# Turns, logits and turned gates of two expert mixtures as 64x64 products, and their second biases inside the chunk sums

## The chip, the cores and the metric

The kernel runs on one core of one Trainium2 chip. The metric is the device time of one launch in microseconds (us), given as the median of several runs. Engines: PE is TensorE, DVE is VectorE, ACT is ScalarE, POOL is GpSimd, SP is SyncE, which issues most of the DMAs.

## What is computed

Two layers on 8 sequences of 1056 tokens (1024 image tokens and 32 text tokens) of width 64: a token embedding, an attention, a first mixture of experts, a recurrent memory ("recall") in place of an attention, and a second mixture of experts. The change is in the mixtures. Layer normalisation of the input precedes each, and the result is added to the input:

```python
gate_scores = jnp.einsum('bsd,ed->bse', x, Wg) + bg
topk_scores, topk_idx = jax.lax.top_k(gate_scores, K)          # K = 2
topk_probs = jax.nn.softmax(topk_scores, axis=-1)
combine = jnp.sum(topk_probs[..., None] * jax.nn.one_hot(topk_idx, E, dtype=x.dtype), axis=-2)
for e in range(E):
    h = jax.nn.relu(jnp.einsum('bsd,hd->bsh', x, W1[e]) + b1[e])
    y = jnp.einsum('bsh,dh->bsd', h, W2[e]) + b2[e]
    out = out + combine[..., e:e + 1] * y
```

The first mixture has E = 16 experts with 128 hidden values, the second E = 8 with 256; the first has the same form, with a normalisation behind it. The last input column is replaced by ones inside the kernel, so that the gate's bias and b1 are the last row of the folded weights. b2 is weighted by the gates, as y is.

## The kernel before

`all_stages` runs the stages in order. `moe_phase` builds a mixture; its names begin with d_ in the first and n_ in the second. Each mixture treats its 8 sequences ("batches") one after another, and each batch in three chunks of 352 tokens (CH). For a chunk the kernel goes through pairs of experts; a pair sits on the two halves of 64 partitions. A unit is one pair, chunk and hidden half of 128: DVE scales the turned tokens by the gates (`scale`, line 1617, into xg), PE makes the hidden values in p_z (`first`, line 1375: four 64x64 products with 352 columns), ACT applies the relu (`relu`, line 1474), PE adds the output into p_y over the eight units of a chunk (`second`, line 1389: again four 64x64 products). A group is two units: `first(i)`, then `second(i - 1)`. A batch has 24 units, 12 groups, and a mixture 96 groups. z(i) below is the first product of group i's `first`. All of it is f32. Behind the last unit of a chunk ACT copies half of p_y into yT (`copy_sum`, line 1481) and DVE adds the other half (`add_half`, line 1602); the next chunk's `second` waits for that.

Between the groups stand the "misc" steps, which share the banks p_g and p_l. Their order is written out by hand: FIRST_GROUP, TURNS, LOGITS, RANK, CHOOSE, KEEP, BIAS_GROUP and OUT_GROUP give the group of each step, `misc_use` numbers them, and a step waits on misc_free until the one before it has been read out, and signals misc_full. On PE a step comes before `first` of its group. For batch b + 1, while batch b is computed, and counted by groups within a batch:
- groups 8, 9, 10: `turn` (line 1334) turns the normalised tokens, which ACT has copied twice side by side (`double`, line 1446), by one 128x128 transpose for each of the nine tiles of 128 tokens, four, four and one of them; ACT copies them into xd (`untangle`, line 1454).
- group 11: `logits` (line 1343), nine products of 64x128 with E columns; DVE ranks in group 0 (`rank`, lines 1539 to 1548), chooses in groups 1 and 2 (`choose`, lines 1554 to 1572).
- group 3: `turn_gates` (lines 1349, 1350), two transposes; ACT keeps the turned gates in cT and cT_text (`keep_gates`), SP writes them to DRAM and reads them back spread over partitions (`spread_out`, `spread_in`, line 1268).
- groups 4 and 5: `turn_out` (line 1364) turns yT of the batch before, five and four transposes; DVE adds the two halves of each to the rows (`add_out`, line 1591).
- group 6: `weigh_biases` (lines 1355, 1356), the turned gates times a block matrix of b2, 512 columns on the whole array and one small product for the text rows; DVE adds that to the rows (`add_biases`, lines 1578, 1579).
DVE also measures and normalises the batch after next in groups 4 to 6 (`measure`, `gather`, `normalise`), and in the first mixture prepares the next stage (feed steps). On DVE, group i's list is: rank, the additions of the turned output, `scale(i + 1)`, `add_half`, biases, `choose`, `measure`.

The first batch's tokens are turned, ranked and chosen in the tail of the stage before: in attention (`attend_stage`) between the last units of the last quad, in bank halves of p_m, on DVE by `gate_first_batch`; in recall (`recall_answer_block`) in the steps behind AFTER, in p_t and p_r.

Of the kernel before, what the change touches and what calls it, by code (L numbers as in the profile page):

```python
# [20 lines left out]
P = 128  # L21
# [566 lines left out]
def attend_stage(g, v_all, own, steps, late_ctx, first):  # L588
# [85 lines left out]
    with ExitStack() as c:  # L674
# [22 lines left out]
        own["p_g"], own["p_l"] = p_m[:, 1, 1, :], p_m[:, 1, 0, :]  # L697
# [183 lines left out]
        def _(dve):  # L881
# [56 lines left out]
            def gate_first_batch():  # L938
# [6 lines left out]
                gather(1)  # L945
                normalise(1)
                keep_weights()
                for k in range(3):
                    untangle(0, k)
# [27 lines left out]
        def _(pe):  # L977
# [126 lines left out]
            for j in range(NQ):  # L1104
# [3 lines left out]
                for u in range(US):  # L1108
# [13 lines left out]
                    if j == NQ - 1 and u in (8, 11, 14):  # L1122
                        turn_tokens(0, (u - 8) // 3)
                    if j == NQ - 1 and u == 17:
                        logits(0)
# [9 lines left out]
            for group in pending:  # L1135
                weigh(*group)

def moe_phase(g, c, pre, E, H, w1_arg, b1_arg, w2_arg, b2_arg, gate_w, gate_b, keep, acc, send, feed, place):
# [17 lines left out]
    bias_added = g.sem(pre + "bias_added")  # L1157
# [14 lines left out]
    order = [(-1, j, "gate", 0, j) for j in (0, 1, 2, 3, 6)]  # L1172
    for b in range(1, B):
        order += [(FIRST_GROUP[b] + at, 0, "gate", b, j) for j, at in enumerate(TURNS + (LOGITS,))] + [(FIRST_GROUP[b] + KEEP, 0, "gate", b, 6)]
    for b in range(B):
        order += [(OUT_GROUP[b] + r, 1, "out", b, r) for r in range(2)] + [(BIAS_GROUP[b], 3, "bias", b, 0)]
# [12 lines left out]

    def bias_use(b):  # L1190
        return misc_use["bias", b, 0]

    def biasing(i):
        return [b for b in range(B) if BIAS_GROUP[b] == i]

# [15 lines left out]
    b2 = sb("b2", [FULL * E, FULL, D])  # L1211
    cT, cT_text = sb("cT", [FULL * E, P]), sb("cT_text", [E, TXT])
# [4 lines left out]
    xn = sb("xn", [P, NT, 2, D])  # L1217
# [3 lines left out]
    is1, is2, cw = (sb(n, [P, NT, E]) for n in ("is1", "is2", "cw"))  # L1221
# [11 lines left out]
    def sync_steps(sp):  # L1233
        def load():
# [7 lines left out]
            for t in range(FULL):  # L1242
                sp.dma_start(b2[t * E:t * E + E, t, :], b2_arg).then_inc(w_in, 16)
# [11 lines left out]
        def spread_out(b):  # L1255
            sp.wait_ge(kept, 2 * b + 2)
            sp.dma_start(c_scr[b, :, 0:TOK].rearrange("e (t p) -> t e p", p=P), cT[:, :]).then_inc(c_sent, 16)
            sp.dma_start(c_scr[b, :, TOK:SEQ], cT_text[:, :]).then_inc(c_sent, 16)
# [30 lines left out]
    def pool_steps(pool):  # L1289
# [3 lines left out]
        def set_ones(pool):  # L1293
            pool.wait_ge(set_up, 1)
            nc.gpsimd.memset(xn[:, :, :, D - 1:D], 1.0).then_inc(set_up, 1)
# [32 lines left out]
    def tensor_steps(pe):  # L1328
        def turn(b, j):
# [3 lines left out]
            for t in range(4 * j, min(4 * j + 4, NT)):  # L1333
                last = nc.tensor.transpose(own["p_g"][:, t % 4 * P:t % 4 * P + P], xn[:, t, :, :].rearrange("p q d -> p (q d)"), g.eye[:])  # L1334
            last.then_inc(misc_full, 1)

        def logits(b):
            pe.wait_ge(misc_free, gate_use(b, 3))
            if b == 0:
                pe.wait_ge(b_in, 16 * (4 + HALVES))  # L1340
            for t in range(NT):
                r, out = slice(t % 2 * D, t % 2 * D + D), (own["p_g"], own["p_l"])[t % 2]
                last = nc.tensor.matmul(out[:, t // 2 * E:t // 2 * E + E], own["xd"][b % 3][r, t * P:t * P + P], gw[r, :], start=True, stop=True)  # L1343
            last.then_inc(misc_full, 1)

        def turn_gates(b):
            pe.wait_ge(misc_free, gate_use(b, 6))
            pe.wait_ge(step, 9 * b + 9)
            nc.tensor.transpose(own["p_g"][0:FULL * E, 0:P], cw[:, 0:FULL, :].rearrange("p t e -> p (t e)"), g.eye[:])  # L1349
            nc.tensor.transpose(own["p_g"][0:E, P:2 * P], cw[:, FULL, :], g.eye[:]).then_inc(misc_full, 1)  # L1350
# [1235 lines left out]
```

## Time and profile before

| | us |
|---|---|
| median of three runs | 1840.27 |
| lowest and highest of them | 1825.12, 1844.62 |
| the profiled execution | 1849.69 |
| its span, first to last instruction | 1847.9 |
| PE busy in that span | 1717.6 |
| DVE, ACT, POOL busy | 1262.4, 1043.6, 358.1 |

The profiled execution is one launch with the hardware profiler on. PE is the product part of TensorE and PEld its weight loads, which run beside products. "Idle before <-" names what ended the idle time ahead of an instruction.
### The profile page before, as it was taken

The page shows a single profiled execution, that of the slowest core. Times are in us where ns is not written, and L with a number is a line of the kernel's source. Part 1 is how long each engine was busy: PE and PEld are TensorE (multiplying, and loading weights), DVE is VectorE, ACT ScalarE, POOL GpSimd, SP SyncE. Part 2 cuts the span into 40 slices and gives each one's busy share as a digit, 9 for nine tenths or more (in the row PEclk, how much of TensorE's full clock was granted, in tenths as well). Part 3 has the DMA queues.
Part 4 walks back from the last instruction along what each step waited for, and adds up shares of the span by engine and source line. Part 5 has one row for each costly group of instructions (what it writes and reads, how often), then busy time and mean ns, then how long its engine had stood idle before and what let it go on. Part 6 is the DMA issues. An engine that isn't in the chain of part 4 may idle for free. (4 is left out here: it accounts for less than half of the span.)

```text
span 1847.9 us, 47299 instructions
## 1 busy us (share of the span) xinstructions
PE 1717.6 (93%) x18586; PEld 744.3 (40%) x18586; DVE 1262.4 (68%) x3205; ACT 1043.6 (56%) x1974; POOL 358.1 (19%) x332
## 2 busy tenths in 40 slices
PE   7978999999999999999898999999999998999999
PEld 3331222222222222222224444445388985444444
DVE  2459888888888888888614688875577654534442
ACT  1330777777777677767645555554533333565554
POOL 2212000000000000000101155546414434000000
PEclk9965999999999999999959999999999998999999
DMA  5742012121212121200215855770120002252241
GB/s 200 264 101 33 8 37 50 36 50 36 50 36 50 31 50 37 44 25 21 48 42 107 169 97 104 142 135 11 38 73 13 2 1 49 57 102 55 55 89 33
DMA packets 89577, 119.20 MB, mean 65 GB/s; under 512 B 31340, under 2 KB 72374, under 8 KB 87310
## 3 DMA queue, kind: packets, MB, share of 16 engines
q1 hardware_dynamic: 84874, 107.28, 27.2%
q0 software_dynamic: 2992, 8.44, 1.3%
q8 instruction: 150, 2.46, 0.6%
q10 hardware_dynamic: 1492, 0.46, 0.1%
q14 instruction: 69, 0.57, 0.1%
HBM read 97.29 MB, written 18.86 MB: 63 GB/s over the span
## 5 line engine op out<-in xcount | busy, mean ns | idle before, releaser
L870 ACT ACTIVATE b_prob<-b_p_s 128x512 f32<-128x512 f32 x1104 | 570.5, 599 | 268.5 <-PE b_p_s L1060 252.4
L893 DVE TENSOR_REDUCE b_m<-b_p_m 128x1 f32<-128x1024 f32 x512 | 603.9, 1219 | 85.2 <-PE b_p_s L1060 65.1
L1088 PE MATMUL b_p_o<-b_prob,v_all 128*9 128x512 f32 x2304 | 310.8, 623 | 1.0
L1474 ACT ACTIVATE d_hidden<-d_p_z 128x704 f32<-128x704 f32 x192 | 135.7, 756 | 96.3 <-PE d_p_z L1375 95.5
L1474 ACT ACTIVATE n_hidden<-n_p_z 128x704 f32<-128x704 f32 x192 | 135.1, 755 | 89.0 <-PE n_p_z L1375 87.6
L1060 PE MATMUL b_p_s<-b_q,b_k 51*64 51x512 bf16 x1024 | 181.2, 415 | 3.3 <-ACT b_prob L870 3.3
L1001 PE MATMUL b_p_m<-b_qk 48*64 48x512 bf16 x856 | 162.7, 441 | 21.9 <-ACT b_prob L870 5.4
L1060 PE MATMUL b_p_s<-b_qk 51*64 51x512 bf16 x1024 | 177.5, 401 | 2.2 <-ACT b_prob L870 2.2
L848 POOL DMA_DIRECT2D sum_scr<-b_sums x46 | 25.3, 550 | 716.7 <-ACT b_sums L860 630.1
L1001 PE MATMUL b_p_m<-b_k,b_q 48*64 48x512 bf16 x800 | 137.2, 392 | 12.2 <-ACT b_prob L870 6.5
L1375 PE MATMUL d_p_z<-d_xg,d_w 64*64 64x352 f32 x1536 | 138.2, 472 | 3.8 <-DVE d_xg L1617 3.0
L1375 PE MATMUL n_p_z<-n_xg,n_w 64*64 64x352 f32 x1536 | 135.0, 467 | 0.4 <-ACT n_hidden L1474 0.2
L1389 PE MATMUL d_p_y<-d_hidden,d_w 64*64 64x352 f32 x1536 | 133.0, 460 | 0.0
L1389 PE MATMUL n_p_y<-n_hidden,n_w 64*64 64x352 f32 x1536 | 131.3, 457 | 0.0
L1001 PEld LDWEIGHTS b_p_m<-b_qk 48*64 48x64 bf16 x856 | 38.5, 111 | 188.0 <-DVE b_m L893 123.2
L1001 PEld LDWEIGHTS b_p_m<-b_k,b_q 48*64 48x64 bf16 x800 | 35.1, 104 | 164.5 <-DVE b_m L893 98.6
L1617 DVE TENSOR_TENSOR d_xg<-d_xd,d_c_wide 128x352 f32<-128x352 f32 x120 | 70.9, 633 | 42.0 <-PEq L674 28.2
L1389 PEld LDWEIGHTS d_p_y<-d_hidden,d_w 64*64 64x64 f32 x1536 | 59.7, 134 | 57.0 <-DVE d_yT L1602 6.7
L1389 PEld LDWEIGHTS n_p_y<-n_hidden,n_w 64*64 64x64 f32 x1536 | 57.6, 133 | 57.5 <-DVE n_yT L1602 7.6
L1375 PEld LDWEIGHTS d_p_z<-d_xg,d_w 64*64 64x64 f32 x1536 | 54.1, 133 | 53.6 <-issue 14.2
L1375 PEld LDWEIGHTS n_p_z<-n_xg,n_w 64*64 64x64 f32 x1536 | 53.8, 133 | 47.8 <-issue 6.4
L1001 PE MATMUL b_p_m<-b_k_head,b_q_head 48*64 48x512 bf16 x392 | 67.0, 405 | 6.3 <-ACT b_prob L870 4.6
(394 smaller groups left out, 2417.0 us busy)
## 6 DMA issues: line engine op xcount, KB each, us to landing
d_c_wide<-d_c_scr SPq DMA_DIRECT2D x40, 704.0 KB, 12.3
m_x_all<-n_c_scr SPq DMA_DIRECT2D x48, 352.0 KB, 8.1
xt<-in_x SPq DMA_DIRECT2D x16, 1024.0 KB, 10.5
sum_scr<-b_sums POOLq DMA_DIRECT2D x31, 256.0 KB, 2.5
qk_scr<-a_qk_part SPq DMA_DIRECT2D x24, 256.0 KB, 2.9
b_qk<-d_c_scr SPq DMA_DIRECT2D x8, 704.0 KB, 19.1
k_rate<-rate_scr SPq DMA_DIRECT2D x8, 528.0 KB, 4.3
b_qk<-qk_scr SPq DMA_DIRECT2D x56, 66.0 KB
```

The costliest lines, as they stand in the source:

```text
L848: pool.dma_start(g.sum_scr[b, p, :, a * WIDE:a * WIDE + w], sums[:, n % 2, 0:w]).then_inc(sum_sent[n % 2], 16)
L870: nc.scalar.activation(prob[:, U % PR_RING, 0:w], p_s[:, U % S_RING, 0:w], ACT.Exp, scale=float(D) ** -0.5).then_inc(exp_done, 1)
L893: nc.vector.tensor_reduce(m3[:, x, 0:1], p_m[:, s, :, :].rearrange("p k n -> p (k n)"), axis=AX.X, op=ALU.max).then_inc(rows_free, 1)
L1001: last = nc.tensor.matmul(out[e:e + 64, k, :], q[:, t * P + e:t * P + e + 64], keys[:, k * WIDE:k * WIDE + WIDE], start=True, stop=True)
L1060: last = nc.tensor.matmul(out[e:e + 64, :], k_st[s][r, q, jt * P + e:jt * P + e + 64], q_st[s][r, q, a * WIDE:a * WIDE + WIDE], start=True ...
L1088: last = nc.tensor.matmul(p_o[32 * i:32 * i + DH + 1, :], v[:, jt, p * QUAD + i, :], prob[:, slot, :], start=(jt == 0), stop=(jt == TILES[ ...
L1375: last = nc.tensor.matmul(own["p_z"][h * D:h * D + D, n % 2, q, 0:CH], w1[r, pr, cols:cols + D], own["xg"][r, n // HALVES % XR, :], start= ...
L1389: last = nc.tensor.matmul(own["p_y"][q * D:q * D + D, h, 0:CH], w2[r, 2 * pr + q, f, :], own["hidden"][r, n % HR, q, :], start=(k == 0), s ...
L1474: nc.scalar.activation(own["hidden"][:, n % HR, :, :], own["p_z"][:, n % 2, :, 0:CH], ACT.Relu).then_inc(relu_done, 1)
L1617: nc.vector.tensor_tensor(own["xg"][:, j % XR, :], own["xd"][b % 3][:, a * CH:a * CH + CH], own["c_wide"][b % 2][a][:, pr, :], ALU.mult)\
```

## The change

- `turn`, `turn_out` and `turn_gates` no longer use transposes of 128x128. Each tile of 128 tokens is turned by four products with a 64x64 identity, on the four 64x64 tiles of the array, and the two halves go into two banks, p_w. The normalised tokens are no longer doubled. The tokens are turned in two steps, of five and four tiles, no longer three.
- `logits` makes two 64x64 products for each tile of tokens where it made one of 64x128.
- Ranking and choosing come one group earlier; turned gates stay in their group.
- `weigh_biases` and DVE's `add_biases` go. In their place PE adds the b2 term to a chunk's sum in p_y: `add_biases(b, a)`, three or four products for each chunk, in the chunk's second unit, with the turned gates as the moving operand.
- cT has two buffers, b2 its rows at the partitions of the turned gates, cw spare columns of zeros.
- In attention's tail PE waits for the folded weights before the first turn, and DVE copies them ahead of the second batch's normalising. In recall's tail, ranking, choosing and turned gates move up by one step.

The core of the diff:

```diff
-    BIAS_GROUP = [5] + [first + 10 for first in FIRST_GROUP[1:]]
-    TURNS, LOGITS, RANK, CHOOSE, KEEP = (0, 1, 2), 3, 4, (5, 6), 7
+    TURNS, LOGITS, RANK, CHOOSE, KEEP = (0, 1), 2, 3, (4, 5), 7
...
-            for t in range(4 * j, min(4 * j + 4, NT)):
-                last = nc.tensor.transpose(own["p_g"][:, t % 4 * P:t % 4 * P + P], xn[:, t, :, :].rearrange("p q d -> p (q d)"), g.eye[:])
+            for k, t in enumerate(TURN_TILES[j]):
+                for q, h in HALF_OF:
+                    r = slice(h * D, h * D + D)
+                    last = nc.tensor.matmul(own["p_w"][q * D:q * D + D, h, k * D:k * D + D], xn[r, t, :], g.eye[r, r], start=True, stop=True,
+                                            skip_group_check=True)
...
-                r, out = slice(t % 2 * D, t % 2 * D + D), (own["p_g"], own["p_l"])[t % 2]
-                last = nc.tensor.matmul(out[:, t // 2 * E:t // 2 * E + E], own["xd"][b % 3][r, t * P:t * P + P], gw[r, :], start=True, stop=True)
+                for h in range(2):
+                    k, r, at = t % 2, slice(t % 2 * D, t % 2 * D + D), t * P + h * D
+                    last = nc.tensor.matmul(own["p_w"][h * D:h * D + D, k, t // 2 * E:t // 2 * E + E], own["xd"][b % 3][r, at:at + D], gw[r, :],
+                                            start=True, stop=True, skip_group_check=True)
...
-        def weigh_biases(b):
-            pe.wait_ge(misc_free, bias_use(b))
-            pe.wait_ge(kept, 2 * b + 2)
-            nc.tensor.matmul(own["p_g"][:, 0:FULL * D], cT[:, :], b2[:, :, :].rearrange("r t d -> r (t d)"), start=True, stop=True)
-            nc.tensor.matmul(own["p_l"][0:TXT, 0:D], cT_text[:, :], b2[0:E, 0, :], start=True, stop=True).then_inc(misc_full, 1)
+        def add_biases(b, a):
+            if a == 0:
+                pe.wait_ge(kept, 2 * b + 2)
+            for k, (t, lo, hi, at) in enumerate(ROWS_OF[a]):
+                q, h = k % 2, t // 4 % 2
+                r = slice(h * D, h * D + D)
+                rows, block = (cT[r, b % 2, at:at + hi - lo], b2[r, t, :]) if t < FULL else (cT_text[r, b % 2, :], b2[r, 0, :])
+                nc.tensor.matmul(own["p_y"][q * D:q * D + D, h, lo:hi], block, rows, start=False, stop=False, skip_group_check=True)
...
                 pe.wait_ge(relu_done, n + 1)
+                if k == 1:
+                    add_biases(b, a)
...
-            for t in range(5) if r == 0 else range(5, NT):
-                bank, k = (own["p_l"], 0) if t == 4 else (own["p_g"], t % 5)
-                last = nc.tensor.transpose(bank[:, k * P:k * P + P], own["yT"][:, t * P:t * P + P], g.eye[:])
+            for k, t in enumerate(TURN_TILES[r]):
+                for h, q in HALF_OF:
+                    rows, at = slice(q * D, q * D + D), t * P + h * D
+                    last = nc.tensor.matmul(own["p_w"][h * D:h * D + D, q, k * D:k * D + D], own["yT"][rows, at:at + D], g.eye[rows, rows],
+                                            start=True, stop=True, skip_group_check=True)
...
+TURN_TILES = [range(0, 5), range(5, NT)]
```

## Rows read from the trace of the kernel before

**Rows 1.** Part 1 of the page of before, whole span

```profile
PE 1717.6 (93%) x18586; PEld 744.3 (40%) x18586; DVE 1262.4 (68%) x3205; ACT 1043.6 (56%) x1974; POOL 358.1 (19%) x332
```

**Rows 2.** Busy time in four stretches (us): mixtures one and two, one middle batch of each

```profile
core 0: us, PE busy (x) PEld busy (x) DVE busy (x) ACT busy (x) POOL busy (x), PEclk, DMA share, GB/s
979.00:1290.00 311.00, 295.08 (x3419) 146.71 (x3419) 228.81 (x1018) 164.71 (x264) 140.76 (x117) 0.99 0.59 112
1150.00:1187.60 37.60, 35.66 (x428) 17.26 (x426) 31.58 (x150) 21.01 (x34) 21.64 (x18) 1.00 0.63 118
1554.00:1848.00 294.00, 285.26 (x3391) 140.43 (x3389) 123.64 (x595) 164.89 (x264) 19.17 (x17) 0.99 0.31 62
1709.70:1745.70 36.00, 35.45 (x427) 17.38 (x426) 16.49 (x82) 21.15 (x34) 2.19 (x2) 1.00 0.35 71
```

**Rows 3.** Timeline of PE in the second mixture, a middle batch

```profile
start us, us, engine line op out<-in xcount [idle before <-releaser]
...
1709.71 1.41 PE L1375 MATMUL n_p_z<-n_xg,n_w 64*64 64x352 f32 x16
...
1716.05 1.41 PE L1375 MATMUL n_p_z<-n_xg,n_w 64*64 64x352 f32 x16
...
1719.20 1.12 PE L1355 MATMUL n_p_g<-n_b,n_cT 64*128 64x512 f32 x2 [0.55 <-DVEq L1597]
...
1720.48 1.42 PE L1375 MATMUL n_p_z<-n_xg,n_w 64*64 64x352 f32 x16
...
1722.89 1.36 PE L1375 MATMUL n_p_z<-n_xg,n_w 64*64 64x352 f32 x16
...
1731.86 1.41 PE L1375 MATMUL n_p_z<-n_xg,n_w 64*64 64x352 f32 x16
...
1735.59 1.42 PE L1375 MATMUL n_p_z<-n_xg,n_w 64*64 64x352 f32 x16
...
1738.01 1.36 PE L1375 MATMUL n_p_z<-n_xg,n_w 64*64 64x352 f32 x16
...
1740.38 1.36 PE L1375 MATMUL n_p_z<-n_xg,n_w 64*64 64x352 f32 x16
...
1745.73 0.53 PE L1375 MATMUL n_p_z<-n_xg,n_w 64*64 64x352 f32 x4
```

**Rows 4.** Timeline of PE in the first mixture, around the turned gates

```profile
1146.48 0.30 PE L1349 MATMUL d_p_g<-eye,d_cw 128*128 128x128 f32 x1 [1.26 <-DVE d_cw L1572]
```

**Rows 5.** Timelines of PE and PEld, small products of the token stage

```profile
28.80 0.86 PE L346 MATMUL a_p_b<-a_wq,t_xT 64*32 64x64 f32 x64
...
28.79 0.70 PEld L346 LDWEIGHTS a_p_b<-a_wq,t_xT 64*32 64x32 f32 x64
```

**Rows 6.** Timeline of PEld, 64x64 weight loads, a product line's start

```profile
1088.04 0.21 PEld L1375 LDWEIGHTS d_p_z<-d_xg,d_w 64*64 64x64 f32 x8 [0.18 <-ACT d_hidden L1474]
```

**Rows 7.** Timeline of PE, two of the 64x128 logits instructions of mixture two

```profile
1734.74 0.25 PE L1343 MATMUL n_p_g<-n_gw,d_xn_all 64*128 64x8 f32 x1
1734.85 0.25 PE L1343 MATMUL n_p_g<-n_gw,d_xn_all 64*128 64x8 f32 x1
```

**Rows 8.** Timeline of DVE in the second mixture, around a chunk's end

```profile
1716.64 0.52 DVE L1602 TENSOR_TENSOR n_yT<-n_yT,n_p_y 128x352 f32<-128x352 f32 x1 [1.72 <-ACT n_yT L1481]
...
1719.30 0.53 DVE L1617 TENSOR_TENSOR n_xg<-d_xn_all,m_x_all 128x352 f32<-128x352 f32 x1 [0.21 <-DVE hid L1591]
```

**Rows 9.** Timeline of DVE in the second mixture, first and last of choosing's seven

```profile
1572.83 0.17 DVE L1554 CAST n_at<-n_top_at 128x18 f32<-128x18 uint32 x1 [0.21 <-DVE hid L1579]
...
1573.68 0.23 DVE L1565 TENSOR_TENSOR n_is<-n_is,n_wt 128x72 f32<-128x72 f32 x1
```

**Rows 10.** Timeline of DVE, start of the first mixture

```profile
991.82 0.96 DVE L1617 TENSOR_TENSOR d_xg<-d_xd,d_c_wide 128x352 f32<-128x352 f32 x2 [7.66 <-DMA d_c_wide<-d_c_scr]
```

**Rows 11.** Busy time, attention's tail: columns as in the second group

```profile
918.70:969.90 51.20, 51.20 (x233) 10.34 (x228) 7.18 (x44) 24.52 (x49) 0.54 (x1) 0.50 0.23 50
969.90:979.00 9.10, 6.79 (x146) 2.46 (x142) 0.11 (x1) 6.05 (x13) 0.15 (x1) 1.00 0.09 32
```

More of the change, by code:

```diff
@@ L945, in gate_first_batch @@
                 gather(1)
+                keep_weights()
                 normalise(1)
-                keep_weights()
-                for k in range(3):
+                for k in range(len(TURN_TILES)):
                     untangle(0, k)
@@ L1121, in _ @@
                         fold_weights()
-                    if j == NQ - 1 and u in (8, 11, 14):
+                    if j == NQ - 1 and u == 8:
+                        pe.wait_ge(own["w_copied"], 3)
+                    if j == NQ - 1 and u in (8, 11):
                         turn_tokens(0, (u - 8) // 3)
-                    if j == NQ - 1 and u == 17:
+                    if j == NQ - 1 and u == 14:
                         logits(0)
@@ L1188, in join_use @@
         return misc_use["join", B - 1, 0]
[L1190 to L1194, printed above, removed]
     def gating(i, k):
@@ new lines, in turn_gates @@
+            for q, h in HALF_OF:
+                r, cols = slice(h * D, h * D + D), q * D % (FULL * E)
+                nc.tensor.matmul(own["p_w"][q * D:q * D + D, h, 0:D], flat_cw[r, cols:cols + D], g.eye[r, r], start=True, stop=True, skip_group_check=True)
+            nc.tensor.matmul(own["p_w"][0:D, 0, D:D + TXT], flat_cw[0:D, FULL * E:FULL * E + D], g.eye[0:D, 0:TXT], start=True, stop=True,
+                             skip_group_check=True).then_inc(misc_full, 1)
+        def add_biases(b, a):
[6 more added lines that the diff above has]
+                nc.tensor.matmul(own["p_y"][q * D:q * D + D, h, lo:hi], block, rows, start=False, stop=False, skip_group_check=True)
@@ L1424, in main @@
                         join_last()
-                    for b in biasing(i):
-                        weigh_biases(b)
                     first(i)
@@ L1452, in untangle @@
             act.wait_ge(misc_full, gate_use(b, j) + 1)
-            n = 512 if j < 2 else P
-            copy(own["xd"][b % 3][:, 512 * j:512 * j + n], own["p_g"][:, 0:n]).then_inc(misc_free, 1)
+            tiles = TURN_TILES[j]
+            copy(own["xd"][b % 3][:, tiles[0] * P:tiles[0] * P + len(tiles) * P].rearrange("p (t h n) -> p h t n", h=2, n=D),
+                 own["p_w"][:, :, 0:len(tiles) * D].rearrange("p h (t n) -> p h t n", n=D)).then_inc(misc_free, 1)
         def soften(b):
@@ L1535, in rank @@
             if part == 0:
-                dve.wait_ge(misc_full, gate_use(b, 3) + 1)
-                for r, bank in enumerate((own["p_g"], own["p_l"])):
+                dve.wait_ge(misc_full, gate_use(b, 2) + 1)
+                for r in range(2):
                     n = (NT + 1 - r) // 2
-                    nc.vector.tensor_copy(logit[:, r::2, :], bank[:, 0:n * E].rearrange("p (t e) -> p t e", e=E)).then_inc(looked, 1)
+                    nc.vector.tensor_copy(logit[:, r::2, :], own["p_w"][:, r, 0:n * E].rearrange("p (t e) -> p t e", e=E)).then_inc(looked, 1)
                 dve.wait_ge(looked, 2 * b + 2)
@@ L1644, in main @@
                         join_last()
-                    for b in biasing(i):
-                        add_biases(b)
                     for part, k in enumerate(CHOOSE):
@@ L2356, in _ @@
                     double(1)
-                if n == AFTER + 7:
+                if n == AFTER + 6:
                     soften(0)
```

117 lines of the change are left out of this document (55 added, 62 removed).

## The prediction

> **What bounds the kernel now.** The page's first part comes first: PE is busy for 93% of the span and no other engine reaches 70% [rows 1]. The table by stage comes second: in the two mixtures PE is busy for 295.08 of 311.00 us and 285.26 of 294.00 us, at a granted clock of 0.99, and in one middle batch of each for 35.66 of 37.60 us and 35.45 of 36.00 us [rows 2]. There a microsecond of PE saved is one of span, until another engine's order of work gets in the way. DVE is the next one, with 31.58 of 37.60 us in the first mixture's batch and 16.49 of 36.00 in the second's.
>
> Then PE's timeline, which is to be read by the starts of the first products (line 1375). A group with nothing else in it lasts 1740.38 - 1738.01 = 2.37 us [rows 3]. Twelve of them would be 28.4 us; the middle batch of the second mixture takes 1745.73 - 1709.71 = 36.0 us. What fills the other 7.6 us, in that batch [rows 3]:
> - two turns of the output: 1716.05 - 1709.71 - 2 x 2.37 = 1.60
> - second biases: 1720.48 - 1716.05 - 2.37 = 2.06, of which 0.55 is a wait for DVE
> - three turns of the tokens: 1731.86 - 1722.89 - 3 x 2.37 = 1.86
> - logits: 1735.59 - 1731.86 - 2.37 = 1.36
> - turned gates, with a wait for a chunk sum: 1745.73 - 1738.01 - 3 x 2.37 = 0.61, of which I give 0.44 to the gates and 0.17 to the chunk.
> - twice 0.05 in the group after a change of form.
> The first mixture's batch has 1.6 us more [rows 2], mostly a wait of 1.26 us for the chosen gates [rows 4].
>
> **The change, part by part.** I count PE instructions as pairs of one weight load and one product. A product of f32 operands gives two such pairs (64 pairs for the 32 text products [rows 5]; 16 for the two units of four products of line 1375 [rows 3]).
>
> *The price of a 64x64 pair with 64 columns.* No row shows this form. From below: sixteen pairs with 352 columns on four 64x64 tiles take half of 2.37 us, 74 ns each, so 64 columns would be 74 x 64 / 352 = 13.5 ns if the four tiles stay busy. Eight weight loads of 64x64 lie within 0.21 us although one takes 0.13 of it, so loads on the four tiles run side by side too [rows 6]. The nearest row in size is that of the token stage: 64 pairs with 64 columns, on 64x32 tiles, in 0.86 us with the last one's tail, whose loads lie within 0.70 us, 11 ns a pair [rows 5]. From above: the logits' 64x128 pairs take 1734.85 - 1734.74 = 0.11 us for two, 55 ns each [rows 7]; between them lies 27 ns, if the two tiles over the same rows shared the loading. I take 14 ns, by rows 5 and 6.
>
> *Per batch, at 14 ns:*
> - turns of tokens: 9 tiles x 4 products x 2 = 72 pairs, 1.01 us for 1.86
> - logits: 9 x 2 x 2 = 36 pairs, 0.50 for 1.36
> - turned gates: 5 x 2 = 10 pairs, 0.14 for 0.44
> - turns of the output: 72 pairs, 1.01 for 1.60
> - second biases: 11 products, 22 pairs, in three pieces. The fullest tile gets 224, 128 and 192 of a chunk's columns; a column costs 2.37 us / 2 / 4 / 352 x 2 = 1.69 ns for a product's two instructions, so 544 columns are 0.92 us if nothing overlaps, and 0.45 us if the 1056 columns spread evenly over four tiles. I take 0.80 for 2.06.
> - the 0.05 twice goes, since nothing in the loop changes the form any more.
> Sum: 3.46 us for 7.42, where nothing waits. The same terms hold in the first mixture.
>
> *What is late next.* The waits now hidden under the biases and turns come out. PE's bias step moves away, and with it a 2.06 us group in which DVE catches up. In group 5 of a batch DVE adds the chunk's half, measures, adds the second half of the turned output and only then scales the tokens for the group after: from z(17) at 1716.05 to the end of that scaling is 1719.30 + 0.53 - 1716.05 = 3.8 us [rows 3, 8]. The next first products would start 2.37 + 0.25 (a bias piece) after z(17), so PE waits 1.15 us. Choosing moves up by a group, behind the addition of a chunk's half: 0.6 us from the products' start until that addition starts [rows 3, 8], 0.5 for it, 1.0 us of choosing (seven operations from 1572.83 to 1573.9 [rows 9]) and 0.5 of scaling make 2.6 us against 2.37, a wait of 0.3, and 0.45 in the first mixture, where choosing and scaling are longer. In exchange its gates are there one group earlier and the 1.26 us wait [rows 4] goes. In the first mixture I add 0.4 us for normalising, which comes through POOL. The chunk wait of 0.17 stays. Together 1.6 us in the second mixture and 2.2 in the first.
>
> New batches: 28.44 + 3.46 + 1.6 = 33.5 us for 36.0, and 28.44 + 3.46 + 2.2 = 34.1 for 37.6. Either mixture has six whole middle batches: 6 x 2.5 + 6 x 3.5 = 36 us.
>
> *The ends.* In the first mixture's first batch DVE stands 7.66 us until a DMA brings the wide gates at 991.8 us [rows 10]: what is saved ahead of it (three turns and logits) is absorbed, and later steps of that batch save 6 us, since choosing gets out of the way. The second mixture's first batch has no such wait: 4.5 us. The last batches, which have only output turns left and now carry their own biases, give 0.5 us together. In attention's tail and in the recall stage's tail the third turn and most of the logits' time goes, among products of other forms, so no change of form is saved: 2 and 1 us.
>
> DVE loses the two bias additions of each batch, POOL and SP nothing; ACT's copy before the turns halves. None of them sets the end of a group, PE's products cover them, and I cost them at nothing; without that cover DVE's waits are those worked out above, and they are in the sum. The added wait for the folded weights in attention's tail is met by moving their copies ahead: nothing.
>
> Sum: 36 + 6 + 4.5 + 0.5 + 3 = 50 us off the profiled execution's 1849.7 us: 1799.7. The median of the runs shown, 1840.3, lies 9.4 below that execution, so the median to expect is 1790.
>
> **The rivals.** *Tiles that share their loading, 27 ns a pair.* 190 pairs a batch x 13.5 ns = 2.6 us, over some 15 batches 38 us given back: 1828. For it: no row has four 64x64 tiles with so few columns. Against it: rows 5 and 6. The Trainium skill (TensorE: Matmul & The Clock Gate, "Wait, 56ns, not 53.3ns?" in Part 1) says that starts of products never come closer than about 25 ns, however small they are; by that rule 190 x 11 ns x 15 = 31 us would be given back, an estimate of 1821. This case's trace does not agree: the 64 pairs of rows 5 start 11 ns apart.
>
> *The same instructions, four times as many: slower.* Where one transpose stood there are eight pairs. If a pair cost what the logits' pairs cost, 55 ns [rows 7], the 190 pairs would take 7.7 us more a batch, 115 us in all, and the result would be 1905. It decides from 14 + 50 / (190 x 15) = 31 ns a pair on. Against it: those pairs load 128 columns each and use two tiles, these load 64 and use four.
>
> *The clock in attention's tail.* From 918.70 to 969.90 us the granted clock was 0.50, that is 1.2 GHz [rows 11], after PE had stood and waited between turns. PE was busy all through it; at twice the clock that work is 25.6 us, and with the busy share of the next stretch, where the clock is 1.00 and PE works 6.79 of 9.10 us, it would take 34: 17 us less, 1773. The change shortens those waits, which is for it; the tail's own rhythm stays, which is against it. One of the three runs shown is 15 us below the median, which would fit.
>
> *DVE's order doesn't bind* where I have it, because the additions of biases that leave it let it get ahead: its waits of 1.15 us a batch shrink to some 0.25, 15 batches x 0.9 = 13 us less, 1777.
>
> **How the numbers follow.** Forecast 0.57, clock 0.15, DVE not binding 0.11, shared loading 0.11, slower pairs 0.06. The likeliest gives 1790. The range runs from 1768, a little under the clock's case, to 1828, shared loading; the slow rival and both gains at once are left out. A measurement of this kernel tells about 1% from no change, 18 us: faster than 1822 are the forecast, the clock, DVE and a little of shared loading, 0.84; within 1% most of shared loading, 0.10; slower 0.06.
>
> **What would show it.** In the new profile a plain group is still 2.37 us. A turn of five tiles is 40 pairs within some 0.6 us, not 1.1 or 2.2; the logits 36 pairs in 0.5. A middle batch lasts 33 to 34 us in both mixtures. PE's new waits name the scaling (line of d_xg and n_xg) twice a batch, about 1.1 and 0.4 us. The wait for the chosen gates is gone. The granted clock in the mixtures stays at 0.99. I am wrong if a middle batch is over 35.5 us, or if the waits for DVE are over 3 us a batch, or under 0.5.

## The result, and the profile after

The changed kernel takes 1863.01 us (median of 4 runs, 1859.31 to 1869.38) against 1842.44 of the kernel before (4 runs, 1825.12 to 1845.89): ratio 1.0144, 95% interval 1.0084 to 1.0204. It is slower by 1.4%; 1790 had been predicted, with a range up to 1828. The profiled execution took 1869.38 us. The page's parts 1 and 3 of the changed kernel, which stand against [rows 1]:

```profile
span 1867.6 us, 52627 instructions
PE 1692.5 (91%) x21306; PEld 813.5 (44%) x21306; DVE 1252.5 (67%) x3140; ACT 1034.7 (55%) x1959; POOL 357.8 (19%) x334
...
q8 instruction: 171, 2.80, 0.7%
```

PE has 2720 more products and as many more loads, and is busy for 25 us less in a span 20 us longer. Queue q8 is new to the argument: its packets are of 16 KB, and they bring an engine's own instructions. That these are PE's is read from the counts: the old kernel's 150 packets stand beside 2 x 18586 products and loads, the changed one's 171 beside 2 x 21306, 248 and 249 for a packet.

The table by stage, both mixtures of the changed kernel (columns as in [rows 2]):

```profile
972.50:1303.00 330.50, 291.39 (x4662) 178.00 (x4654) 226.86 (x985) 161.70 (x257) 137.73 (x116) 0.95 0.53 106
1573.60:1862.30 288.70, 270.95 (x4602) 177.42 (x4594) 115.39 (x559) 160.34 (x257) 21.22 (x17) 0.98 0.31 62
```

PE's work did get shorter: 291.39 us where the first mixture had 295.08, although part of it ran at half the clock, and 270.95 where the second had 285.26 [rows 2]. What grew is the time in which it stands, and in the first mixture the clock fell to 0.95. From the first product to the last (line 1390, before 1375) the first mixture lasts 330.5 us for 309.2, the stage between 270.7 for 265.8, and the second mixture 288.6 for 287.9.

What PE stood for, as the view of waits sums it up. The changed kernel, first mixture and then second (the same view of the kernel before has no line with "issue" in either):

```profile
PE d_p_z L1390 <- DVE d_xg L1622: 18.1, 17, 2.9
PE d_p_z L1390 <- issue: 8.1, 4, 3.4
PE d_p_y L1406 <- issue: 6.0, 2, 3.4
PE d_p_w L1348 <- issue: 3.3, 1, 3.3
PE d_p_w L1337 <- issue: 1.5, 1, 1.5
...
PE n_p_z L1390 <- DVE n_xg L1622: 6.7, 6, 1.1
PE n_p_z L1390 <- issue: 6.3, 3, 4.3
PE n_p_w L1348 <- issue: 2.7, 1, 2.7
PE n_p_y L1406 <- issue: 1.6, 1, 1.6
```

"Issue" means that nothing which the profile shows held PE back. It adds up to 18.9 us and 10.6 us, in single stalls of up to 4.3 us, on whatever line PE had reached: in the middle of a row of logits, of first products, of second ones. A wait on a semaphore would sit where the program has it, ahead of the first instruction of a step. One of them, in PE's timeline of the second mixture:

```profile
1708.58 0.81 PE L1337 MATMUL n_p_w<-eye,m_x_all 64*64 64x64 f32 x40
1709.19 1.43 PE L1390 MATMUL n_p_z<-n_xg,n_w 64*64 64x352 f32 x16
...
1711.62 0.64 PE L1337 MATMUL n_p_w<-eye,m_x_all 64*64 64x64 f32 x32
1712.09 1.37 PE L1390 MATMUL n_p_z<-n_xg,n_w 64*64 64x352 f32 x16
...
1714.53 0.73 PE L1348 MATMUL n_p_w<-n_gw,d_xn_all 64*64 64x8 f32 x22
1717.94 0.35 PE L1348 MATMUL n_p_w<-n_gw,d_xn_all 64*64 64x8 f32 x11 [2.68 <-issue]
```

The turn of five tiles starts at 1708.58 and the products behind it at 1709.19: 40 pairs in 0.61 us, as forecast. But between the 22nd and the next of 36 logits pairs PE stands.

Two views of the same place show why. The DMA queues between 1701.9 and 1715.1 us, by kind (packets, MB, share of the 16 engines), and PE's work from 1700.85 to 1715.18 and on to 1718.00:

```profile
q1 hardware_dynamic: 2134, 1.58, 65.7%
q14 instruction: 1, 0.01, 0.2%
```

```profile
1700.85:1715.18 14.33, 13.20 (x258) 7.98 (x254) 7.17 (x30) 8.73 (x14) 2.58 (x2) 1.00 0.62 115
1715.18:1718.00 2.82, 0.14 (x6) 0.06 (x6) 0.00 (x0) 0.00 (x0) 0.00 (x0) 1.00 1.05 216
```

In 13 us no q8 packet starts, while q1 carries the output and the six spreading transfers of the gates (`spread_in`, 2 MB a batch in this mixture, 4 MB in the first). In that time PE takes 258 products and 254 loads, 512 instructions. The next packet starts at 1715.18, and PE goes on at 1717.94, 2.8 us later; until then all engines stand. The same holds for each of the 13 stalls of the two mixtures: PE goes on 2.7 to 3.0 us after a q8 packet has started. This is the plainest sign that what PE lacked was instructions. Where the queues are free, one comes every 250 or so of PE's instructions (228 and 268 in two successive stretches of thin_after below). The kernel before, in its longest stretch of this kind, took 418 and had no stall, nor had it one in the 2.8 us behind (484 by 1733.90):

```profile
1712.59:1731.12 18.53, 17.98 (x208) 8.63 (x210) 10.53 (x38) 11.31 (x17) 2.19 (x2) 1.00 0.48 95
```

The recall stage's tail, where ranking and choosing had been moved up by a step, shows another loss (before, the same wait was 0.62 us):

```profile
1546.25 7.94 PE L2268 MATMUL k_trio<-k_eT,k_yT 128*128 128x64 f32 x36 [4.89 <-DVE k_yT L2392]
```

### The profile page after: what moved, and what is told of

Its sections match the earlier page's. It is cut to its first block and busy times, and to the rows that moved or that the text cites. A ratio compares the mean times of both kernels' runs of the same rounds, so it can differ in the third digit from the quotient of the medians.

```text
span 1867.6 us, 52627 instructions
## 1 busy us (share of the span) xinstructions
PE 1692.5 (91%) x21306; PEld 813.5 (44%) x21306; DVE 1252.5 (67%) x3140; ACT 1034.7 (55%) x1959; POOL 357.8 (19%) x334
## 5 line engine op out<-in xcount | busy, mean ns | idle before, releaser
L1060 PE MATMUL b_p_s<-b_q,b_k 51*64 51x512 bf16 x1024 | 177.2, 405 | 4.7 <-ACT b_prob L870 4.7
L1390 PE MATMUL d_p_z<-d_xg,d_w 64*64 64x352 f32 x1536 | 149.0, 483 | 26.2 <-DVE d_xg L1622 18.1
L1406 PE MATMUL d_p_y<-d_hidden,d_w 64*64 64x352 f32 x1536 | 151.1, 475 | 6.0 <-issue 6.0
L1390 PE MATMUL n_p_z<-n_xg,n_w 64*64 64x352 f32 x1536 | 144.0, 466 | 13.1 <-DVE n_xg L1622 6.7
L1406 PE MATMUL n_p_y<-n_hidden,n_w 64*64 64x352 f32 x1536 | 147.1, 463 | 1.6 <-issue 1.6
L1390 PEld LDWEIGHTS d_p_z<-d_xg,d_w 64*64 64x64 f32 x1536 | 67.0, 139 | 72.6 <-issue 47.3
L1406 PEld LDWEIGHTS d_p_y<-d_hidden,d_w 64*64 64x64 f32 x1536 | 73.2, 138 | 51.6 <-issue 12.5
L1406 PEld LDWEIGHTS n_p_y<-n_hidden,n_w 64*64 64x64 f32 x1536 | 75.0, 134 | 40.6 <-DVE n_yT L1607 9.6
L1390 PEld LDWEIGHTS n_p_z<-n_xg,n_w 64*64 64x64 f32 x1536 | 71.4, 134 | 48.0 <-issue 22.4
L1607 DVE TENSOR_TENSOR n_yT<-n_yT,n_p_y 128x352 f32<-128x352 f32 x24 | 12.5, 522 | 93.6 <-ACT n_yT L1496 93.6
```

The lines of the kernel that those rows point to most:

```text
L1060: last = nc.tensor.matmul(out[e:e + 64, :], k_st[s][r, q, jt * P + e:jt * P + e + 64], q_st[s][r, q, a * WIDE:a * WIDE + WIDE], start=True ...
L1390: last = nc.tensor.matmul(own["p_z"][h * D:h * D + D, n % 2, q, 0:CH], w1[r, pr, cols:cols + D], own["xg"][r, n // HALVES % XR, :], start= ...
L1406: last = nc.tensor.matmul(own["p_y"][q * D:q * D + D, h, 0:CH], w2[r, 2 * pr + q, f, :], own["hidden"][r, n % HR, q, :], start=(k == 0), s ...
L1607: nc.vector.tensor_tensor(own["yT"][:, cols], own["yT"][:, cols], own["p_y"][:, 1, 0:CH], ALU.add).then_inc(sum_copied, 1)
```

## The experiments

Theory F: TensorE takes its instructions faster than they are brought while the spreading fills the DMA queues; the number of instructions and the traffic are both needed. Its rivals: the new products themselves or their banks (B), the amount moved rather than its bunching (M), VectorE's order (D). All ratios are to the kernel before, run beside each. Stage lengths are from each run's one profiled execution. paced, spaced, the versions with the old turns and those of VectorE's order but the first have recall_order's edit too, so their measure is its 1855 us and not the changed kernel's 1863 (with the thin spreading, thin_after's 1820 less the same 5 to 8 us).

### Traffic away, in the changed kernel and in the old one

```diff
+                    if b >= 2:
+                        sp.dma_start(own["c_wide"][b % 2][a][q * D:q * D + D, 0:1, 0:8], ...).then_inc(c_in[b % 2][a], 16)
+                        continue
```

> The changed kernel, but from the third batch of each mixture on the spreading of the gates over the partitions moves 8 columns of one pair instead of 352 columns of all pairs (so those gates are stale: part of the computation is left out). Theory F (PE runs out of instructions: its 16 KB refills wait behind the spreading's packets while the many short pairs of turns and logits use up what is buffered): the gaps of 2 to 4.8 us in PE's stream disappear in batches 2 to 7, the refills come about every 250 PE instructions, the clock drops in the mixtures go, and the time falls by 30 to 45 us against the changed kernel, to about 1820 to 1833. Theory W (the new waits for DVE's scaling and choosing are what costs): these are untouched, the time falls by under 8 us. Theory P (the small products themselves are dear): under 8 us.

> The same cut of the spreading in the kernel before. Theory F: its PE instructions last through the spreading, so it gains little: 0 to 8 us (1835 to 1842). If the spreading costs either kernel something else (memory ports, late gates), the gain is the same as in the changed kernel, over 20 us.

Measured: changed 1819.88 us (1818.6 to 1821.92, 4 runs), ratio 0.9896 (0.9855 to 0.9937); old 1829.02 (10 runs), 0.9973 (0.9927 to 1.0019). So the traffic costs the changed kernel some 43 us and the old one nothing that can be told. In the changed kernel the first mixture goes from 330.5 to 300.1 us, the second from 288.6 to 274.2; all waits for issue are gone. So is most of the time at half the clock: the clock's records give 40 us of it in the two mixtures of the changed kernel and 11 in the thin one. The 30 us less at half the clock are worth 15 us; with the 29.5 us of waits that is the 44.8 us by which the mixtures are shorter. In the old kernel the mixtures stay at 310.6 and 288.0. A middle batch of each mixture of the thin changed kernel, by stretches:

```profile
1158.50:1195.20 36.70, 33.41 (x600) 20.04 (x601) 31.36 (x145) 20.41 (x33) 21.83 (x19) 1.00 0.02 5
1694.90:1728.90 34.00, 32.87 (x604) 20.23 (x596) 15.64 (x79) 20.30 (x33) 2.58 (x2) 1.00 0.06 12
```

The second one is near the forecast of 33.5; the first is 2.6 us above its 34.1.

### The number of instructions alone, in the old kernel

```diff
+            if b >= 1 and j < 2:
+                for k in range(5):
+                    for q, h in HALF_OF:
+                        r = slice(h * D, h * D + D)
+                        nc.tensor.matmul((own["p_g"], own["p_l"])[h][q * D:q * D + D, k * D:k * D + D], w1[r, 0, 0:D], g.eye[r, r], ...)
```

In pad_double `range(5)` is gone through twice in the second mixture; thin_pad_double is pad_double with the edit above.

> The old kernel with 40 more pairs of 64x64 products (their results are overwritten) ahead of each of the first two turns of a batch, from the second batch on: 28 such pads, 1120 more multiplies, where the change has 2720 more. Own price at the 15 ns a pair of the changed kernel's turns: 28 x 0.6 = 17 us, so about 1857 to 1860 from the old kernel's 1840. Theory F (TensorE outruns the supply of its instructions while the gates' spreading fills the DMA queues): the number of instructions alone makes the stalls, so gaps of 2 to 4 us with a late 16 KB refill appear inside the batches of both mixtures, and the time is 1870 to 1895. Rival B (the stalls belong to the new products into two banks, to the new bias products or to their waits): no gap over 1.8 us inside a batch, and 1855 to 1862.

> The old kernel with the padding of the run pad_before, and twice as much of it in the second mixture. There, pad_before took at most 380 instructions of TensorE between two refills in the saturated stretch and had no stall; the changed kernel takes 440 to 520 and has stalls of 2 to 5 us. 160 more instructions a batch before its end would make some 450 to 500. Own price of the added products 7 us, so 1881. Theory F: stalls appear in the second mixture, 5 to 20 us more: 1886 to 1900. Rival B: 1878 to 1884 and no gap over 1.8 us inside a batch of the second mixture.

> The kernel of pad_double with the thin spreading (the later batches' gates are others). Own price of the padding: 28 x 0.6 + 12 x 0.6 = 24 us on the thin old kernel's 1829. Theory F (stalls need both the instructions and the traffic): 1848 to 1856, and no stall over 1.8 us inside the second mixture's batches. Rival B (the products cost by themselves): the 1914 of pad_double less the 9 us that the thin spreading gave the old kernel, so about 1900 to 1906.

Measured: pad_before 1874.07 us (4 runs), ratio 1.0168 (1.0117 to 1.0219); pad_double 1914.4, 1.0372 (1.0313 to 1.0431); thin_pad_double 1866.7 (10 runs), 1.0127 (1.0080 to 1.0174). The second mixture is the clean case. The stretch from its first product to its last, in pad_before, pad_double and thin_pad_double:

```profile
1568.10:1862.90 294.80, 290.61 (x3903) 149.62 (x3903) 120.98 (x582) 165.19 (x264) 18.86 (x17) 1.00 0.31 61
```

```profile
1580.90:1905.10 324.20, 306.04 (x4424) 161.88 (x4423) 120.44 (x571) 165.56 (x264) 18.99 (x17) 0.98 0.28 55
```

```profile
1559.40:1861.20 301.80, 297.61 (x4424) 156.90 (x4423) 119.85 (x575) 165.24 (x264) 18.85 (x17) 1.00 0.08 17
```

The old kernel takes 287.9 us there. Half the padding adds 6.9, its own price. All of it adds 13.9 without the traffic, its own price again, and 36.3 with it: 22.4 us come only where both meet: 14.0 us of waits for issue, and some 16 us at half the clock, worth 8. What PE waited for in that stretch of pad_double (thin_pad_double has no such line):

```profile
PE n_p_g L1337 <- issue: 7.1, 2, 3.7
PE n_p_l L1337 <- issue: 3.8, 1, 3.8
PE n_p_z L1381 <- issue: 3.1, 2, 1.7
```

None of the change is in this kernel. Rival B falls. The first mixture, whose traffic lasts 20 us of a batch, stalls with half the padding already (8.5 us of issue waits). Two expectations were missed: pad_before was to stall in both mixtures and did so in the first alone, and pad_double came out 14 us above its range. thin_pad_double came out 10 us above what I expected: its mixtures account for what they should (320.1 us for thin_before's 310.6 in the first, 13.8 more in the second); in the profiled executions the rest lies in stages that the padding doesn't touch. 14.5 us of it are ahead of the first mixture, where the clock was at half for 24 us in thin_pad_double and for 3 in thin_before, with the same code there; why the clock differs is not shown.

### The traffic moved or spread out

```diff
-                if send and it >= 1:
-                    send_out(it - 1)
                 if it + 1 < B:
                     spread_out(it + 1)
                     spread_in(it + 1, range(NC))
+                if send and it >= 1:
+                    send_out(it - 1)
```

> The changed kernel with SP sending the finished batch out behind the spreading of the next gates, not ahead of it, in the second mixture (the first doesn't send). The spreading then runs some 3 groups earlier, in groups 4 to 8 of a batch and not in 8 to 11 with the turns and logits. Theory F: the long gaps in PE's stream of the second mixture go or shrink to under a third, 10 to 18 us in all; the first mixture stays as it is. Theories W and P: no change (within 4 us).

Measured 1852.06 us (10 runs), 1.0079 (1.0043 to 1.0115). The second mixture goes from 288.6 to 276.5 us, its waits for issue from 10.6 to 1.7: the same bytes are issued 12.0 us ahead of the turns of the tokens and no longer 2.0 to 2.5, and in a middle batch the last one lands 2.5 us after the turns begin and not 12.7.

```diff
+                    if at:
+                        sp.wait_ge(gated, at + 2 * a + q)
```

That is paced, with `at` the batch's third count; spaced has `at + 4 * a + 2 * q` from the fourth on.

> The changed kernel with the recall tail's old order, and each of the six spreading transfers of a batch issued only as VectorE has scaled one group more (counts 3 to 8 of the batch), instead of all at once. Same bytes, same packets. Theory F: the DMA queues have gaps in which refills come through, so in the second mixture, where the six take 11 us together, the stalls of 2 to 5 us go (-8 to -12 us), and in the first, where they take about 20 us of a batch, some do (-5 to -15 us): 1830 to 1842. Rival M (what costs is bytes moved, not their bunching, or SyncE comes too late): within 5 us of 1855, or columns' gates late at a chunk's start.

> The changed kernel with the recall tail's old order, and the six spreading transfers issued at counts 4, 6, 8, 10, 12 and 14 of the batch's scaled groups, so some 6 us apart. The pacing of the run before opened no gap (its transfers were as long as a group, and in the second mixture all six had fallen due before the first was issued); 6 us are longer than one transfer (1.8 us in the second mixture, 3.4 in the first). Theory F: the DMA queues are empty a third of the time or more, refills come on time, the stalls of both mixtures mostly go (44 us of them in the changed kernel): 1855 to between 1815 and 1835. Rival M (the bytes cost, not their bunching): within 5 us of 1855.

Measured: paced 1855.11 us, 1.0072 (1.0036 to 1.0109); spaced 1854.02, 1.0088 (1.0060 to 1.0117); nothing gained, I had expected 1815 to 1842. Neither tests what it was made for, because most counts had been passed when the first transfer was issued. In a middle batch of spaced four of the six go out within 2.5 us in either mixture; in the first all six are out after 8 us and the last has landed after 25, and in the second the last two come 5 and 13 us behind the fourth, so that only the sixth stands apart. The stalls lie in the block of the others. The stretch ahead of one in the second mixture, from one refill to the next (476 instructions; PE stands for 2.2 us and goes on 3.1 us after that refill has started):

```profile
1647.27:1661.17 13.90, 12.77 (x241) 7.08 (x235) 7.41 (x30) 8.73 (x14) 2.58 (x2) 1.00 0.55 97
```

### Fewer instructions in the changed kernel

```diff
-                for q, h in HALF_OF:
-                    last = nc.tensor.matmul(own["p_w"][q * D:q * D + D, h, k * D:k * D + D], xn[r, t, :], g.eye[r, r], ...)
+                last = nc.tensor.transpose(own["p_w"][:, k // 4, k % 4 * P:k % 4 * P + P], xn[:, t, :, :].rearrange("p q d -> p (q d)"), g.eye[:])
```

The tokens are doubled again for it, and old_turns has recall_order's edit (below). The others add the old form of the logits, spaced's edit, and the thin spreading.

> The changed kernel with the recall tail's old order, and the tokens turned by 128x128 transposes again (in two steps of five and four tiles); logits, gates and biases stay new. Against the 1855 us of the changed kernel with the old recall order. By their own price the turns are 0.4 to 0.6 us a batch dearer, 6 to 8 us over 14 batches. Theory F: some 50 fewer pairs a batch, and dearer ones, leave the refills more time, so part of the 30 + 14 us of stalls goes: 1835 to 1852 in all. Rival B (stalls not from the number of instructions): 1861 to 1864.

> The run with the tokens' turns as before (1826), and the logits as 64x128 products again. By their own price old logits are a tenth of a us dearer a batch or equal (the prediction had 0.5 us for the new ones). Theory F with supply already enough in that run: 1824 to 1832. Rival N (each reduction of pairs keeps helping): below 1820.

> The run with the tokens' turns as before (1826) and the same spacing of the spreading. In that run only some 4 us of late refills were left in the first mixture and none in the second. Theory F: 1820 to 1826, hardly a gain, since its TensorE doesn't outrun its supply. If it gains over 8 us, the spreading costs in another way too.

> The kernel of the thin spreading (1820; from the third batch on only 8 columns of one pair are spread, so the output of those batches is of other gates) with the recall tail's old order (-6) and the tokens' turns as before. With the supply no longer in question, the turns show their own price: theory F and the prediction's prices have the old turns 0.4 to 0.6 us a batch dearer, so 1820 to 1823 against 1814 for the new turns. If it is 1814 or below, the new turns bring nothing even where supply is free, because VectorE's waits take their place.

Measured: old_turns 1826.06 us (1823.98 to 1828.02, 4 runs), 0.9899 (0.9850 to 0.9948); old_turns_logits 1831.1, 0.9962 (0.9924 to 1.0000); old_turns_spaced 1824.53, 0.9921 (0.9886 to 0.9955); thin_old_turns 1824.54, 0.9921 (0.9884 to 0.9959). A transpose of 128x128 is one pair, the four products that replaced it are eight, so old_turns has 63 pairs fewer a batch. It gains 29 us on recall_order (below), more than expected (1835 to 1852), though its turns are dearer. Its waits for issue are 3.0 and 1.2 us. The solid stretch of its second mixture, from one refill to the next:

```profile
1700.52:1714.12 13.60, 13.19 (x205) 7.83 (x200) 5.49 (x37) 8.82 (x13) 1.58 (x1) 1.00 0.84 163
```

405 instructions, at a fuller DMA share than that of the stall, and a stall of 0.6 us follows, by when there are 444. With the thin spreading the old turns cost 305.0 and 278.1 us in the mixtures for 300.1 and 274.2: what the new ones are worth where the supply holds is 8.8 us, 0.6 a batch, in one execution of each. The logits' form makes no difference that can be told.

### VectorE's order

```diff
-                if n == AFTER + 5:
+                if n == AFTER + 6:
                     rank(0, 0)
+                    rank(0, 1)
+                    choose(0, 0)
```

> The changed kernel with DVE's ranking and choosing in recall's tail put back behind the gating of the last recall answers. Theory R (they delay the last gatings, so PE waits 4.9 us for k_yT in recall's tail): that wait falls under 1 us and recall's stage is about 5 us shorter; the whole 4 to 7 us faster than the changed kernel, 1857 to 1859. Otherwise nothing changes there.

Measured 1854.96 us (7 runs), 1.0082 (1.0045 to 1.0119), 8 us less than the changed kernel (4 to 7 expected); between the mixtures 265.4 us for 270.7, and the wait is 1.20 us for 4.89:

```profile
1541.86 5.79 PE L2268 MATMUL k_trio<-k_eT,k_yT 128*128 128x64 f32 x36 [1.20 <-DVE k_yT L2392]
```

```diff
+            scale(1)
...
-                    if i + 1 < TG:
-                        scale(i + 1)
+                    if i + 2 < TG:
+                        scale(i + 2)
```

> The changed kernel with the recall tail's old order, and VectorE scaling two groups ahead instead of one (the ring of scaled columns is long enough). Theory D: in the first mixture VectorE's side work (statistics, ranking, adding out) stands ahead of scaling, and TensorE now waits 1.2 + 1.8 + 1.3 us a batch for scaled columns, in the second 1.2 us; with a group more of lead these go: 2 to 4 us a batch of the first and 1 of the second, 1855 - 18 to 30 = 1825 to 1837. Rival T (VectorE has no throughput to spare, or the wait moves to another step of its chain, or the supply of instructions takes the time instead): within 5 us of 1855.

> The same with the full spreading (the changed kernel's work, all of it). Theory F: what VectorE's order gives, the supply partly takes back, since TensorE reaches the same number of instructions in the same saturated stretch sooner: 1838 to 1850, with stalls of 2 to 5 us still in most batches. If the gain of VectorE's order comes through in full, 1830 to 1835.

> The thin spreading (the later batches' output is of other gates), the recall tail's old order, VectorE scaling two groups ahead, and statistics, normalising and ScalarE's copy for the turns each one group earlier. No supply stalls and no late columns. Theory D (VectorE's order is the second missing term, 16 us in the first mixture, 7 in the second): from some 1814 down to 1790 to 1800, with batches of 34 to 35 us in the first mixture and 32.5 to 33.5 in the second. Rival T (VectorE has no throughput to spare, so the wait turns up elsewhere): 1809 to 1816.

> All that was learnt: logits, gates and biases new, the tokens' turns as before, the recall tail's old order, VectorE two groups ahead with statistics and normalising a group earlier, and the sending of a batch's output behind the spreading. Theory F and D: from 1826 down by 8 to 20 us, to 1806 to 1818. Rival T: 1822 to 1830.

Measured: ahead 1851.95 us (10 runs), 1.0053 (1.0009 to 1.0098); shift 1850.76, 1.0074 (1.0040 to 1.0108); thin_shift 1833.32, 0.9953 (0.9922 to 0.9983); best 1841.72 (12 runs), 1.0007 (0.9977 to 1.0036). Theory D's cure fails: ahead was to reach 1837 or less, thin_shift 1800 and best 1818, and the last two lie above the ranges of both theories. `best` is slower than old_turns by 16 us. Against thin_after the first mixture of thin_shift is 19 us longer, the second 2.6 shorter. The wait only moves. In ahead's second mixture PE no longer waits for scaled columns but, at the same total, for what stands in line behind normalising:

```profile
PE n_p_w L1337 <- ACT m_x_all L1461: 7.0, 5, 1.6
```

In the first mixture of `best` ScalarE, whose copy for the turns had been moved up as well, waits for VectorE with the relus in line behind it, and PE for ScalarE:

```profile
PE d_p_z L1387 <- ACT d_hidden L1486: 18.1, 7, 3.1
PE d_p_y L1403 <- DVE d_yT L1604: 8.0, 7, 1.6
```

## Why the prediction was wrong

On the profiled execution, 1869.4 us stand against a forecast of 1799.7, 69.7 more. The stages, measured less forecast, give it:

- **The spreading's stalls, 44.8 us.** 30.4 in the first mixture and 14.4 in the second, changed kernel less thin one: 29.5 us of waits for issue, and 30 us more at half the clock, worth 15. The step that failed is "There a microsecond of PE saved is one of span, until another engine's order of work gets in the way", together with the counting itself: a pair was priced at 14 ns of TensorE's time, and bringing it, on queues that the spreading fills, had no term. No rival had it: the "four times as many" one took the pairs to be slow, and they are not.
- **The first mixture's batches, about 16 us, 11 of them VectorE's order.** A batch takes 36.7 us with the supply free, not 34.1. Some 1.9 of the 2.6 us are VectorE's, read against the same groups of the second mixture: the group behind choosing takes 1.3 us more, for which "What is late next" has 0.45; the last group of a batch takes 1.2 us more, for which it has nothing, since the ranking that now stands there was left out; and the wait for the normalised tokens is 0.2 where it has 0.4. The other 0.7 us are products: with the changes of group the 40 pairs of a turn add 0.74 us and the 32 add 0.53, 17 to 18 ns a pair. VectorE is busy for 31.36 of those 36.7 us, and the groups without other work for PE meet its side work. In that last group it runs statistics (1.2 us), then ranking (3.1), and only then scales; PE waits:

```profile
1190.27 1.23 DVE L1765 BATCH_NORM_STATS2 f_st<-d_xn_all 128x6 f32<-128x64 f32 x9
...
1191.91 0.79 DVE L1562 MAX8 d_top<-d_logit 128x8 f32<-128x16 f32 x9
...
1194.52 0.94 DVE L1626 TENSOR_TENSOR d_xg<-d_xd,d_c_wide 128x352 f32<-128x352 f32 x2
```

```profile
1195.17 1.42 PE L1394 MATMUL d_p_z<-d_xg,d_w 64*64 64x352 f32 x16 [1.02 <-DVE d_xg L1626]
```

  That these waits lie there is read from the trace; that another order would save them was tried in four versions and not found.
- **The recall tail, 5.9 us.** "2 and 1 us" saved; it lost 4.9, as recall_order shows. I had costed the products there and not what ranking and choosing do to the last gatings when they stand ahead of them on VectorE.
- **The rest of the mixtures, some 8 us less saved than forecast**: 2 in the first; 6 in the second, of which 3 are its middle batches, 34.03 us for 33.5 (the products above cost 0.8 us more, the 0.3 us wait for choosing did not come), and 3 its ends.
- **Attention's tail, 5.2 us the other way.** Its half-clock stretch is shorter (924.6 to 948.5 us for 918.7 to 969.9 [rows 11]) and it ends 7.2 us earlier, where 2 had been forecast. The record shows no more than luck in that: in the executions whose code is the old one up to the first mixture that stretch lasts 51, 3, 24, 51 and 24 us (before, thin_before, pad_before, pad_double, thin_pad_double), and the mixture starts anywhere from 958.7 to 983.1 us. The other versions have 20 to 24 us, and one has 44. The clock rival is not borne out by it.

44.8 + 16 + 5.9 + 8 - 5.2 = 69.5.

What was right: the price of a pair, nearly. 40 in 0.61 us is 15 ns for 14; rows 5 and 6 were the right rows. The Trainium skill (TensorE: Matmul & The Clock Gate, "Wait, 56ns, not 53.3ns?" in Part 1) has starts at least 25 ns apart; that would be 1.0 us for the 40, and the trace does not show it. The plain group stays at 2.37 us, the 1.26 us wait for the chosen gates is gone, and the wait behind the turned output is 1.1 us, six times in the second mixture, for the forecast 1.15 (the line of n_xg in the view of waits above). The clock in the mixtures, which was to stay at 0.99, did not, and with the stalls gone (thin_after) it was back at 0.99 or above. Around one of them in the first mixture of the changed kernel:

```profile
1171.00:1174.90 3.90, 0.66 (x16) 0.56 (x7) 3.13 (x22) 0.00 (x0) 2.53 (x3) 0.86 1.10 205
1174.90:1180.30 5.40, 5.38 (x60) 4.09 (x64) 4.10 (x31) 1.51 (x2) 5.09 (x5) 0.50 0.25 47
```

PE stood for 3.3 us and then worked for 5.4 us at 0.50, the 1.2 GHz level.

Open: why the refill is late. It may be asked for late or wait behind q1's packets; no run here tells that. Nor was a version made in which all six transfers come apart, so whether their bunching or their amount matters (rival M) stays open too; that their place matters send_late shows.

## What to carry to other kernels

Price an instruction twice, once in the engine's time and once as something that has to be brought: pairs of 15 ns ran TensorE dry here, after some 430 to 530 instructions without a refill in a stretch of DMA traffic. That count is no threshold: the kernel before took 484 without a stall, old_turns stood for 0.6 us after 444, and behind a refill that had itself come late the changed kernel stood again after 255. That stretch of its first mixture, between two refills:

```profile
1209.49:1218.54 9.05, 5.54 (x129) 4.38 (x126) 3.63 (x23) 3.66 (x6) 0.40 (x1) 1.00 1.10 222
```

Before replacing one instruction by eight, look at where the packets of the instruction queues lie in the DMA view and what traffic the new ones will run beside; issuing that traffic some 10 us earlier gave back 12 of the second mixture's 14 us. And when work leaves an engine's groups, list for each group what the next engine does before it delivers: an average of busy time hides it, and moving one step ahead in an order with few idle gaps moves the wait with it.

Of the versions that compute everything, those that keep the old turns of the tokens beat both kernels: old_turns with 1826.06 us, 1.0% under the kernel before (0.5 to 1.5%) and 37 us under the changed one, and old_turns_spaced with 1824.53, 0.8% under (0.5 to 1.1%); old_turns_logits is 0.4% under, at the edge of its interval.

## What was not expected of the hardware

- TensorE's instructions arrive in packets of 16 KB, one for about 250 instructions, on a DMA queue of their own, and they come late beside the kernel's own traffic: none for 14 us at a mean DMA share of 0.55 to 0.84. The stall comes after 512 instructions in the changed kernel, 476 in spaced and 448 in pad_double, whose stretch since the last refill reads:

```profile
1643.00:1652.70 9.70, 8.92 (x228) 5.69 (x220) 3.53 (x7) 5.95 (x9) 1.07 (x1) 1.00 0.74 127
```

  The Trainium skill (Runtime: NRT & Kernel Launch, "Instruction fetch mechanics") describes the 16 KB blocks of 256 instructions, which agrees with the 250 seen. It holds the fetching to be hidden, since instructions are dispatched more slowly than they are brought; here it was not, in the runs that have both many short instructions and full DMA queues (29.5 us of waits in the changed kernel).
- Padding that costs its own price twice (6.9 us for 560 products, 13.9 for 1120) costs nothing more for the first half and 22 us more for the second once the traffic is there: the effect does not grow in proportion to the instructions.
